# A top-2 expert stage: pairs of blocks in a pipeline of two, with one block of transposes a pair

## The reference

```python
B, S, H, M, E, K = (4, 1024, 512, 2048, 8, 2)
logits = jnp.einsum('bsh,eh->bse', x, Wr)
probs = jax.nn.softmax(logits, axis=-1)
top_v, top_i = jax.lax.top_k(probs, K)
top_v = top_v / jnp.sum(top_v, axis=-1, keepdims=True)
for e in range(E):
    w_e = jnp.sum(jnp.where(top_i == e, top_v, 0.0), axis=-1)
    h = jax.nn.gelu(jnp.einsum('bsh,mh->bsm', x, W1[e]) + b1[e], approximate=False)
    y = jnp.einsum('bsm,hm->bsh', h, W2[e]) + b2[e]
    out = out + y * w_e[..., None]
```

## Time and profile before

| what | us |
|---|---|
| three runs: median (lowest to highest) | 2728.38 (2727.69 to 2734.23) |
| span of the profiled execution | 2727.7 |
| PE busy in it | 2445.3 (90%) |
| L3021, busy | 231.3 |
| L3043, busy | 226.8 |
| L3076 on ACT, busy | 112.0 |

### The profile page before, as it was taken

One profiled execution on the slowest core, in us unless ns is written; L12 is line 12 of the kernel. 1 busy time (PEld: TensorE's weight loads), 2 busy tenths in 40 slices (PEclk: granted clock), 3 DMA queues, 4 the chain that ended last, 5 costly groups with the idle time before them and its releaser, 6 DMA issues. The chain is left out here.

```text
span 2727.7 us, 31762 instructions
## 1 busy us (share of the span) xinstructions
PE 2445.3 (90%) x11965; PEld 1236.3 (45%) x11965; DVE 1375.3 (50%) x1957; ACT 919.0 (34%) x1861; POOL 645.2 (24%) x523
## 2 busy tenths in 40 slices
PE   7799999889999999897599799886998679999996
PEld 4344444334555555545355454353675333333332
DVE  5689999521778886732336512286444521111114
ACT  3555565303533334501122110086333212222221
POOL 0477887401000000001201100000000024444332
PEclk9999999989999999998799799998998889999998
DMA  3632222335535444334620000022000162560634
GB/s 107 204 105 89 75 83 92 98 127 209 179 125 179 158 151 116 131 110 163 194 91 0 22 21 3 20 75 93 1 1 4 55 251 95 203 269 26 244 108 142
DMA packets 96587, 301.31 MB, mean 110 GB/s; under 512 B 27018, under 2 KB 57446, under 8 KB 81724
## 3 DMA queue, kind: packets, MB, share of 16 engines
q1 hardware_dynamic: 62784, 171.06, 18.9%
q0 software_dynamic: 33664, 128.35, 13.0%
HBM read 446.13 MB, written 47.22 MB: 181 GB/s over the span
## 5 line engine op out<-in xcount | busy, mean ns | idle before, releaser
L749 POOL TENSOR_TENSOR x_rows<-ms_state,mb_C_everywhere 128x800 f32<-128x800 f32 x128 | 246.8, 1936 | 165.9 <-DVE ms_state L719 133.0
L774 PE MATMUL psum<-mb_context,mb_key_w 128*128 128x361 f32 x768 | 269.5, 490 | 16.5 <-ACT x_rows L633 10.2
L1005 PE MATMUL psum<-at_Wv,at_context 128*128 128x512 f32 (+1 forms) x576 | 265.0, 599 | 0.0
L719 DVE TENSOR_TENSOR_SCAN ms_state<-ms_decay,psum 128x800 f32<-128x800 f32 x128 | 233.0, 1820 | 19.1 <-ACT ms_decay L666 14.3
L3076 ACT ACTIVATE tf_hidden<-psum,tf_b 128x64 f32<-128x64 f32 x512 | 112.0, 330 | 363.7 <-PE psum L3032 363.7
L3021 PE MATMUL psum<-tf_W,tf_x_T 128*64 128x512 f32 x1024 | 231.3, 599 | 0.8 <-DVE tf_x_T L3085 0.8
L3043 PE MATMUL psum<-tf_W,tf_hidden 128*64 128x512 f32 x1024 | 226.8, 595 | 0.0
L774 PEld LDWEIGHTS psum<-mb_context,mb_key_w 128*128 128x128 f32 x768 | 140.1, 193 | 148.4 <-ACT x_rows L633 43.2
L2956 POOL DMA_INDIRECT tf_W<-in_L_W,tt_weight_row x120 | 119.8, 999 | 180.8 <-PE psum L3021 123.2
L1106 ACT ACTIVATE at_prob<-psum,at_neg_max 100x722 f32<-100x722 f32 x128 | 110.5, 864 | 144.9 <-DVE at_neg_max L1168 144.7
L1168 DVE TENSOR_REDUCE at_neg_max<-psum 100x1 f32<-100x722 f32 x128 | 115.5, 903 | 79.5 <-PE psum L1026 79.2
(11 more groups left out here) (481 smaller groups left out, 3819.8 us busy)
## 6 DMA issues: line engine op xcount, KB each, us to landing
at_piece<-in_L_W_f POOLq DMA_DIRECT2D x24, 1024.0 KB, 6.4
keys_dram<-x_rows SPq DMA_DIRECT2D x128, 180.5 KB, 1.9
at_k_cols<-keys_dram SPq DMA_DIRECT2D x64, 361.0 KB, 3.2
sf_W<-in_L_W SPq DMA_DIRECT2D x16, 1024.0 KB, 7.0
tf_W<-in_L_W SPq DMA_DIRECT2D x8, 2048.0 KB, 20.3
mb_context<-in_ctxT SPq DMA_DIRECT2D x16, 541.5 KB, 4.3
at_context<-in_ctxT SPq DMA_DIRECT2D x8, 1083.0 KB, 5.0
ternary_dram<-at_piece_made POOLq DMA_DIRECT2D x14, 512.0 KB, 4.0
```

Source lines behind the costliest of these rows:

```text
L719: nc.vector.tensor_tensor_scan(state[:, n % RH, :], decay[:, g % RA, :, :].rearrange("p b l -> p (b l)"), drive, 0.0, ALU.mult, ALU.add).t ...
L749: nc.gpsimd.tensor_tensor(seen[:, n % RV, :], state[:, n % RH, :], cC[:, n, :], ALU.mult).then_inc(weighed, 1)
L774: last = nc.tensor.matmul(side("key", u, t == KE - 1)[:, 0:SH], lhsT=wk[:, k, e * P:(e + 1) * P], rhs=keys[:, h, k, :], start=(k == 0), st ...
L1005: last = nc.tensor.matmul(bank[0:rows_of(t), :], lhsT=ctxT[:, b % 2, k, t * P:t * P + rows_of(t)], rhs=wv[:, k, h * BANK:(h + 1) * BANK], ...
```

## The change

The pairs become a pipeline of two. TensorE's order is now U0 U1 U2 U3 of pair p, then one block of transposes (x of p + 1, and all four chunks of p), then D of pair p - 1. In the last pair D of pair 14 stands behind U0 of pair 15. `hid` and `u` are doubled (the second ones lie in the space of the layer's input columns `c.xT`, which is free by then), the turned chunks have four banks, and the second layer has one bank in place of two, so that D of p waits for the b2 add of p - 1. GpSimd's b2, second-layer weights and y rows come one pair later (`take_down`), and x of p + 1 waits for one more x to be turned.

```diff
-    hid = sb("hidden", [P, KM, P])
+    spare = c.xT[:, :, :].rearrange("p k t -> p (k t)")
+    hid = [sb("hidden", [P, KM, P])[:, :, :], spare[:, 0:KM * P].rearrange("p (m t) -> p m t", m=KM)]
+    u = [sb(f"up_{n}", [P, BANK])[:, :] for n in range(2)] + [spare[:, KM * P + n * BANK:KM * P + (n + 1) * BANK] for n in range(2)]
-    up, turned, down, x_bank = c.banks[0:2], c.banks[2:4], c.banks[4:6], c.banks[6]
+    up, turned, down, x_bank = c.banks[0:2], [c.banks[i] for i in (2, 3, 4, 7)], c.banks[5], c.banks[6]
# GpSimd
+        def take_down(p):
+            if p >= 2:
+                pool.wait_ge(y_ready, p - 1)
+            take_b2(p)
+            for h in range(2):
+                pool.wait_ge((half_down, down_filled)[h], 2 * p)
+                if h == 1:
+                    give(p - 1)
+                for z in range(2):
+                    take(w2_half(z, h), dram[f"L1_W2_{h}"], z, p, w2_loaded[h])
         for p in range(1, NPAIR):
-            if p >= 2:
-                give(p - 2)
             for h in range(2):
                 pool.wait_ge(up_filled, 2 * ((p - 1) * NCH + (h + 1) * HC))
                 ...
             if p + 1 < NPAIR:
-                pool.wait_ge(x_turned, p)
+                pool.wait_ge(x_turned, p + 1)
                 take_x(p + 1)
             ...
             if p >= 2:
-                pool.wait_ge(y_ready, p - 1)
-            take_b2(p)
-            ...
+                take_down(p - 1)
+        take_down(NPAIR - 1)
# TensorE
         turn_x(0)
         for p in range(NPAIR):
-            raise_up(p, 0)
-            raise_up(p, 1)
-            turn_up(p, 0)
-            raise_up(p, 2)
-            turn_up(p, 1)
-            raise_up(p, 3)
-            if p + 1 < NPAIR:
-                turn_x(p + 1)
-            turn_up(p, 2)
-            bring_down(p, 0)
-            turn_up(p, 3)
-            for n in range(1, NCH):
-                bring_down(p, n)
+            for n in range(NCH):
+                raise_up(p, n)
+                if p == NPAIR - 1 and n == 0:
+                    down_pair(p - 1)
+            turn_pair(p)
+            if 0 < p < NPAIR - 1:
+                down_pair(p - 1)
+        down_pair(NPAIR - 1)
# in turn_up, bring_down, scalar
-            if t >= 2:
-                pe.wait_ge(gelued, t - 1)
+            if p:
+                pe.wait_ge(gelued, t + 1 - NCH)
-            if n == 0 and p >= 2:
-                pe.wait_ge(y_ready, p - 1)
+            if n == 0 and p:
+                pe.wait_ge(y_ready, p)
-            if p:
-                act.wait_ge(down_filled, 2 * p)
+            if p >= 2:
+                act.wait_ge(down_filled, 2 * (p - 1))
# VectorE
+        choose, weigh = early
         take_turned(0)
         for p in range(NPAIR):
             for n in range(NCH):
+                copy_up(p, n)
+                if p == NPAIR - 1 and n == 0:
+                    add_bias(p - 1)
             if p + 1 < NPAIR:
                 take_turned(p + 1)
-            if p >= NPAIR - 2:
-                early[p - NPAIR + 2](dve)
+            if 0 < p < NPAIR - 1:
+                add_bias(p - 1)
+            if p == NPAIR - 2:
+                choose(dve)
+        weigh(dve)
+        add_bias(NPAIR - 1)
```

More of the change, by code:

```diff
@@ L2918, in top2_ffn @@
     w1, w2, b1 = each("W1", [P, NCH, KD, BANK]), each("W2", [P, KM, D]), each("b1", [P, KM])
[L2919 to L2920 removed]
+    x, xT, y, b2 = each("x", [P, D]), each("x_T", [P, KD, P]), each("y", [P, D]), each("b2", [P, D])
+    spare = c.xT[:, :, :].rearrange("p k t -> p (k t)")
+    hid = [sb("hidden", [P, KM, P])[:, :, :], spare[:, 0:KM * P].rearrange("p (m t) -> p m t", m=KM)]
+    u = [sb(f"up_{n}", [P, BANK])[:, :] for n in range(2)] + [spare[:, KM * P + n * BANK:KM * P + (n + 1) * BANK] for n in range(2)]
     w1_first, w2_first, b1_first = [sem(f"W1_first_{h}") for h in range(2)], [sem(f"W2_first_{h}") for h in range(2)], sem("b1_first")
@@ L3028, in turn_up @@
             pe.wait_ge(up_copied, t + 1)
-            if t >= 2:
-                pe.wait_ge(gelued, t - 1)
+            if p:
+                pe.wait_ge(gelued, t + 1 - NCH)
             for m in range(GM):
-                last = nc.tensor.transpose(turned[t % 2][:, m * P:(m + 1) * P], u[t % 2][:, m * P:(m + 1) * P], c.ident[:, :])
+                last = nc.tensor.transpose(turned[n][:, m * P:(m + 1) * P], u[n][:, m * P:(m + 1) * P], c.ident[:, :])
             last.then_inc(up_turned, 1)
@@ L3038, in bring_down @@
                 pe.wait_ge(w2_loaded[n // HC] if p else w2_first[n // HC], 32 * max(p, 1))
-            if n == 0 and p >= 2:
-                pe.wait_ge(y_ready, p - 1)
+            if n == 0 and p:
+                pe.wait_ge(y_ready, p)
             for m in range(n * GM, (n + 1) * GM):
                 for z in range(2):
-                    ins = nc.tensor.matmul(down[p % 2][cols(z), :], lhsT=hid[:, m, cols(z)], rhs=w2[z][:, m, :],
+                    ins = nc.tensor.matmul(down[cols(z), :], lhsT=hid[p % 2][:, m, cols(z)], rhs=w2[z][:, m, :],
                                            start=(m == 0), stop=(m == KM - 1))
@@ L3048, in bring_down, with turn_pair, down_pair @@
                         ins.then_inc(down_filled, 1)
+        def turn_pair(p):
+            if p + 1 < NPAIR:
+                turn_x(p + 1)
+            for n in range(NCH):
+                turn_up(p, n)
+        def down_pair(p):
+            for n in range(NCH):
+                bring_down(p, n)
         turn_x(0)
         for p in range(NPAIR):
-            raise_up(p, 0)
-            raise_up(p, 1)
-            turn_up(p, 0)
-            raise_up(p, 2)
-            turn_up(p, 1)
-            raise_up(p, 3)
-            if p + 1 < NPAIR:
-                turn_x(p + 1)
-            turn_up(p, 2)
-            bring_down(p, 0)
-            turn_up(p, 3)
-            for n in range(1, NCH):
-                bring_down(p, n)
+            for n in range(NCH):
+                raise_up(p, n)
[5 more added lines that the diff above has]
+        down_pair(NPAIR - 1)
     def scalar(act):
@@ L3068, in scalar @@
             act.wait_ge(b1_loaded if p else b1_first, 32 * max(p, 1))
-            if p:
-                act.wait_ge(down_filled, 2 * p)
+            if p >= 2:
+                act.wait_ge(down_filled, 2 * (p - 1))
             for n in range(NCH):
-                t = p * NCH + n
-                act.wait_ge(up_turned, t + 1)
+                act.wait_ge(up_turned, p * NCH + n + 1)
                 for m in range(GM):
                     for z in range(2):
-                        last = nc.scalar.activation(hid[:, n * GM + m, cols(z)], turned[t % 2][:, m * P + z * W:m * P + (z + 1) * W], ACT.Gelu,
+                        last = nc.scalar.activation(hid[p % 2][:, n * GM + m, cols(z)], turned[n][:, m * P + z * W:m * P + (z + 1) * W], ACT.Gelu,
                                                     bias=b1[z][:, n * GM + m:n * GM + m + 1])
@@ L3085, in take_turned, with copy_up, add_bias @@
             nc.vector.tensor_copy(xT[p % 2][:, :, :].rearrange("p k t -> p (k t)"), x_bank[:, 0:KD * P]).then_inc(xT_ready, 1)
[L3087 to L3096, removed]
-            if p >= NPAIR - 2:
-                early[p - NPAIR + 2](dve)
+        def copy_up(p, n):
+            dve.wait_ge(up_filled, 2 * (p * NCH + n + 1))
+            if p:
+                dve.wait_ge(up_turned, (p - 1) * NCH + n + 1)
+            nc.vector.tensor_copy(u[n], up[n % 2]).then_inc(up_copied, 1)
+        def add_bias(p):
             dve.wait_ge(down_filled, 2 * (p + 1))
@@ L3102, in vector @@
                 dve.wait_ge(y_stored[p % 2], 16 * (p // 2))
-            nc.vector.tensor_tensor(y[p % 2][:, :], down[p % 2], b2[p % 2][:, :], ALU.add).then_inc(y_ready, 1)
+            nc.vector.tensor_tensor(y[p % 2][:, :], down, b2[p % 2][:, :], ALU.add).then_inc(y_ready, 1)
+        choose, weigh = early
+        take_turned(0)
+        for p in range(NPAIR):
+            for n in range(NCH):
+                copy_up(p, n)
+                if p == NPAIR - 1 and n == 0:
+                    add_bias(p - 1)
+            if p + 1 < NPAIR:
+                take_turned(p + 1)
+            if 0 < p < NPAIR - 1:
[4 more added lines that the diff above has]
+        add_bias(NPAIR - 1)
     return Parts(sync=sync, gpsimd=gpsimd, tensor=tensor, scalar=scalar, vector=vector, free=Last(w1, up_filled, y_ready, y[(NPAIR - 1) % 2], share_loaded, cleared), stored=y_stored)
```

## The result

| | median us | lowest to highest | runs |
|---|---|---|---|
| before | 2726.13 | 2720.39 to 2734.55 | 22 |
| changed | 2730.93 | 2725.91 to 2738.87 | 22 |

The ratio is 1.0019, with a 95% interval of 1.0011 to 1.0027: the change costs 5.2 us (3.0 to 7.4). Forecast were +2.4 us and 2730.8. That the level fits to 0.1 us is luck: the kernel before has a median of 2726.13 over 22 runs, where the three runs that the forecast started from had 2728.38. The difference is what counts, and it was forecast too small by 2.8: +2.4 lies just under the interval.

The account below looks back on a forecast made before the run. TensorE was taken as the bound, except at the ends, where y's DRAM return finishes last. Pair 14's second layer 3.4 us later, less 1.0 for the store, gave +2.4: span 2730.1, plus 0.7, 2730.8 us; range 2724 to 2738.

Parts of the forecast that it names:

- The seams: TensorE's blocks of transposes: one block in place of four saves 0.90 us a pair, 14.4 us over 16 pairs.
- The hole: Start: TensorE idles 11.9 us before pair 1's first layer, waiting for GpSimd's weight transfer; the clock's fall adds 1.95 us.
- The steady state: Between start and end: Gelu, bias adds and weight transfers add no waits, also where experts change; priced at 0.
- D(14): Second layer of pair 14: ends at 2670.4 against 2666.97 before, 3.4 us later.
- The end: y's way through DRAM still ends last; its store lands in 2.8 us instead of 4.96, of which 1.0 is taken.
- The same order stands after: After pair 14's second layer: y's store and four loads keep their order; that way took 31.5 us before.
- The new wait for Gelu at D(15): Ahead of pair 15's second layer TensorE waits 0.7 us for the first Gelu; y still ends last.
- (A): Rival at the start: no stall before pair 1's first layer, so 2716.9 us, faster; chance 8%.
- (D): Rival at the end: slower y loads or a clock that returns later, +9 us or more, 2738; chance 4%.
- (B): Rival at changes of expert: weights land late and TensorE waits, 15 us with three waits, 2746; chance 6%.
- (C): Rival at the long transpose blocks: the clock falls at each, 29 us in 15 pairs, 2760; chance 4%.

Follow-up runs that it names:

- e4: Changed kernel with the transposes of pairs 1 to 14 put back into four blocks a pair; ratio to the kernel before 1.0144.
- e3: Changed kernel with the second layer of pair 0 ahead of the first layer of pair 1; ratio to the kernel before 0.9980.
- e1: Changed kernel with GpSimd's wait for the stored shares and its gather moved to the start of pair 2's turn; ratio to the kernel before 0.9989.
- e9: e4 with GpSimd asking for b1 behind the second-layer weights instead of ahead of them; ratio to the kernel before 1.0044.
- e2: Kernel before with GpSimd's wait for the stored shares and its gather moved to pair 2's turn; ratio to the kernel before 0.9993.
- e5: Changed kernel with the second layer of pair 14 and its bias add ahead of pair 15's first first-layer chunk; ratio to the kernel before 1.0002.
- e10: Changed kernel with each of the four loads of y cut into 96 and 4 rows; ratio to the kernel before 1.0006.

## Why the prediction was right

**The seams: right.** 0.90 us a pair from the period, 29.95 us, was met to 0.01, and e4's quiet pairs give it back (30.86). Transposes in a block of 20 cost 0.11 as in one of 8. Gain over 16 pairs 14.4.

**The hole: right.** 11.9 us forecast, 11.65 measured; the clock 1.95, measured 16.13 - 13.90 = 2.23. e3 shows by taking it away that it is D(0)'s place that decided. What the prediction did not see is that the wait for the shares is only the larger half of it, 6.6 of 11.65 us: had GpSimd been free, the DMA engines would have held the transfer (e1).

**The steady state: right.** No idle of TensorE in 450 us, none of L3049 for weights. e4 and e9 show what this rested on: the four Gelu of a pair end early in D, and so GpSimd's queue moves. In the changed kernel its request for b1, behind the last Gelu, goes out at 2341.86, 6.5 us into a D of 13.8.

**D(14): right.** Forecast 3.4 us later than before, measured 468.5 - 464.8 = 3.6.

**The end: the term that was mis-sized.** The prediction had the store land in 2.8 (2.74 measured) and took 1.0 us off the way of y. In fact this way grew, from 31.6 to 32.9 us: the four loads took 3.4 us longer. The step that failed is "The same order stands after", with a faster store counted as a gain. The last request for the upper half of pair 15's weights goes out 4.2 us behind the bias add of D(14) in both kernels (at 2671.21 before, 2670.26 now), but the first load of y is issued 0.1 us behind it (2670.38), where it was 2.3 (2673.53). So the loads begin sooner only to share the engines with the upper half for longer, and from 2683 on, alone, they move the same 182 GB/s as before. That the sharing is the cause is argued from these places; no run takes the upper half away. What more runs do show is that the gain isn't there: e3 and e9 have the changed kernel's ending and a store of 2.75, their loads take 25.95 and 25.83 us, and their way of y is 31.7 and 31.6 us, as long as before the change. The growth by 1.3 is not shown, since the way varies by itself, from 30.6 (e2) to 35.4 (e1) us over the kernels with loads of 100 rows. Between the last bias add and the end 1.2 us came back (26.0 to 24.8, the bringing of the rows 8.58 in place of 9.52); this stretch too lies between 24.8 and 26.4 in the kernels with the same work there, so the 1.2 may be chance. Sum: +3.6 + 1.3 - 1.2 = +3.8 (before rounding) by the traces against the forecast 2.4. The median's +5.2 has an interval that holds 3.8; nothing in the traces shows the other 1.4.

**The new wait for Gelu at D(15):** 0.7 forecast, 0.61 measured, and hidden behind y.

**Rivals.** (A), no stall: out. Its price was 13.9 us at the start; e3 is 12.1 ahead there with a wait for Gelu of 1.9 of its own, which bears the price out, and 10.1 at the end. (D), the longer end: its direction is that of the mis-sized term, its +9 was not met. (B): not here, but real (e4). (C): out; the windows over a block of 20 transposes, 2273.11 to 2275.45 of the changed kernel, have the full clock (us, PE, clock, DMA share, GB/s):

```profile
2273.00:2275.00 2.00, 2.00 (x19) 1.00 0.00 0
2275.00:2277.00 2.00, 2.00 (x13) 1.00 0.07 5
```

The Trainium skill's statement in "TensorE: Matmul & The Clock Gate", Part 4, that transposes don't count as busy in the way that matmuls do, is not borne out as a cost at this length between dense matmuls.

## What to carry to other kernels

A pipeline's first turn takes away work that stood over something: look for what each engine's queue was waiting for beside the moved work, also where nothing is transferred but a semaphore is still waited for. A request that waits in order behind a slow one is a dependency, as b1 behind Gelu was; one move in the queue was worth 23 us. Where the last thing is a round trip through DRAM, look at what starts it and at what else each of its transfers waits for: of 2.2 us won at its first step in e5 1.4 arrived, of 6.7 in e1 4.2, of 9.1 in e3 all, while TensorE's own end, 1.0 us later in e5, cost nothing.

## What the runs showed of the hardware that was not expected

- An indirect transfer that moves nothing landed in 2.1 us on idle DMA engines (changed kernel, 2224.91) and in 12 us where some 4.8 MB of other transfers were still to come (e1, 2213.88).
- A hole of 5.03 us (e1) cost TensorE as much clock as one of 11.65: 2.1 and 2.2 us for the 64 records behind it.
- Loads of 100 rows kept 0.64 of the DMA engines busy at 182 GB/s; cut to 96 and 4 rows (e10) they kept all busy at 218 GB/s.
